# An MoE and attention block on one core: the second tile's upper experts moved from step 11 to step 9, their gating from step 11 to step 10

## The reference

```python
xn = _layernorm(x)
# attention: 16 heads of 8 features, causal
q, k, v = (xn @ W.T + b for each of Wq, Wk, Wv)
scores = einsum('bhqd,bhkd->bhqk', q, k) / sqrt(8)
attn = softmax(where(causal, scores, -inf))
a = einsum('bhqk,bhkd->bhqd', attn, v) @ Wo.T + bo
# experts: the best 2 of 8, weighted by the softmax of their two logits
top_val, top_idx = top_k(einsum('btd,ed->bte', xn, gate_w), 2)
y_all = einsum('btd,edm->btem', xn, We)
e = sum(y_all at top_idx * softmax(top_val))
out = x + a + e
```

## Time and profile before

| what | value |
|---|---|
| median of 3 runs | 516.22 us |
| span of the profiled execution | 510.5 us |
| PE busy | 477.8 us, 94% |
| VectorE busy | 420.7 us, 82% |
| ScalarE busy | 396.9 us, 78% |
| GpSimd busy | 345.9 us, 68% |
| share of PE in the chain that ended last | 89% |

### The profile page before, as it was taken

One profiled execution on the slowest core, in us unless ns is written; L12 is line 12 of the kernel. 1 busy time (PEld: TensorE's weight loads), 2 busy tenths in 40 slices (PEclk: granted clock), 3 DMA queues, 4 the chain that ended last, 5 costly groups with the idle time before them and its releaser, 6 DMA issues.

```text
span 510.5 us, 17312 instructions
## 1 busy us (share of the span) xinstructions
PE 477.8 (94%) x6274; PEld 393.8 (77%) x6274; DVE 420.7 (82%) x1111; ACT 396.9 (78%) x1062; POOL 345.9 (68%) x561
## 2 busy tenths in 40 slices
PE   2548799999999999999999999999999999999995
PEld 1437688888888888888888888888888888888863
DVE  5897698888888898888888898888888898888721
ACT  3644688888888888888888888888888888887773
POOL 7264657777777777778777777777777777755443
PEclk9999999999999999999999999999999999999999
DMA  4664746656547566655465566655556566552000
GB/s 124 195 140 117 188 122 152 161 136 156 134 119 162 130 151 156 160 139 145 105 168 128 148 154 160 156 141 143 139 128 147 138 152 161 133 132 44 15 13 22
DMA packets 64281, 67.79 MB, mean 133 GB/s; under 512 B 6828, under 2 KB 59180, under 8 KB 59484
## 3 DMA queue, kind: packets, MB, share of 16 engines
q1 hardware_dynamic: 64196, 66.68, 53.0%
HBM read 44.90 MB, written 21.23 MB: 130 GB/s over the span
## 4 chain that ended last, share of the span: by engine, by line
PE 89%; DVE 3%; ACT 3%; DMA 2%; issue 2%; SPq 0%; POOL 0%; DVEq 0%; POOLq 0%; ACTq 0%
PE m L841 23%; PE oT_ps L911 17%; PE scoreT_ps L887 13%; PE score_ps L867 12%; PE scoreT_ps L892 5%; PE score_ps L861 5%; PE m L953 3%; PE m L996 3%; PE m L1014 3%; PE m L926 2%; PE m L1021 1%; PE m L962 1%; DMA qstack<-mT 1%; ACT probs L499 1%; DVE negmax L625 1%
## 5 line engine op out<-in xcount | busy, mean ns | idle before, releaser
L625 DVE TENSOR_REDUCE negmax<-score_ps 128x2 f32<-128x512 f32 (+1 forms) x384 | 249.7, 678 | 46.4 <-PE score_ps L867 43.7
L499 ACT ACTIVATE probs<-scoreT_ps 128x512 f32<-128x512 f32 x384 | 216.5, 603 | 74.2 <-PE scoreT_ps L887 48.0
L394 POOL TENSOR_TENSOR fours<-lower,upper 128x512 f32<-128x512 f32 x64 | 81.7, 1276 | 54.1 <-ACT upper L549 54.1
L841 PE MATMUL m<-we_hl,xnT_hl 128*128 128x512 f32 x384 | 114.6, 420 | 0.0
L867 PE MATMUL score_ps<-kstack,qstack 72*128 72x128 bf16 (+1 forms) x1024 | 103.8, 224 | 5.6 <-DVE negmax L625 5.5
L887 PE MATMUL scoreT_ps<-qstack,kstack 123*128 123x128 bf16 (+1 forms) x1024 | 102.0, 221 | 3.3 <-DMA qstack<-mT 2.6
L911 PE MATMUL oT_ps<-probs,vaug 128*32 128x256 f32 (+1 forms) x2048 | 96.7, 329 | 0.2 <-ACT probs L499 0.2
L887 PEld LDWEIGHTS scoreT_ps<-qstack,kstack 123*128 123x128 bf16 (+1 forms) x1024 | 68.1, 98 | 26.5 <-ACT probs L499 15.4
L911 PEld LDWEIGHTS oT_ps<-probs,vaug 128*32 128x32 f32 x2048 | 57.3, 109 | 29.1 <-ACT probs L499 0.4
L549 ACT ACTIVATE upper<-m,weight 128x128 f32<-128x128 f32 x256 | 73.1, 376 | 8.2 <-PE m L841 8.2
L867 PEld LDWEIGHTS score_ps<-kstack,qstack 72*128 72x128 bf16 (+1 forms) x1024 | 72.1, 100 | 8.8 <-DVE negmax L625 7.6
(11 more groups left out here) (81 smaller groups left out, 649.7 us busy)
## 6 DMA issues: line engine op xcount, KB each, us to landing
kstack<-scratch SPq DMA_DIRECT2D x93, 192.0 KB
scratch<-parts SPq DMA_DIRECT2D x64, 192.0 KB, 2.4
qstack<-scratch SPq DMA_DIRECT2D x62, 192.0 KB
qstack<-scratch SPq DMA_DIRECT2D x31, 256.0 KB
x_sb<-in_x SPq DMA_DIRECT2D x32, 128.0 KB, 2.3
scratch<-parts SPq DMA_DIRECT2D x32, 128.0 KB, 1.9
out<-out_sb SPq DMA_DIRECT2D x32, 128.0 KB, 3.7
qstack<-mT SPq DMA_DIRECT2D x64, 8.0 KB, 2.1
```

The lines of the kernel that those rows point to most:

```text
L394: g.tensor_tensor(fours[:, :, q, :], lower[:, :, q, :], upper[:, :, q, :], ALU.add).then_inc(pool_sum, 1)
L499: a.activation(o, i, ACT.Exp, scale=SCALE).then_inc(act_exp, 1)
L625: v.tensor_reduce(o, score_ps[n % 2][:].rearrange("p (h k) -> p h k", h=w), axis=AX.X, op=ALU.max, negate=True).then_inc(dve_max, 1)
L841: ins = tn.matmul(o, l, r, start=first, stop=l is low)
```

## The change

Two places change. On PE the product of the upper experts of the second tile, `experts(mix, 3)`, stood in step 11 behind `turn_input` and ahead of the output projection; now it stands in step 9, directly behind `experts(mix, 2)`. It keeps its wait for the first tile's gating by ACT (`act_upper`), which frees bank `m2`. On ACT the gating of that product, `upper_experts(mix, 1)`, stood in step 11 between `copy_input` and `round_input`; now it stands at the head of step 10.

```diff
@@ ACT, slot(t, s) @@
                     if n == 11 and has(s, NXT):
                         copy_input(t + NXT)
-                    if n == 11 and has(s, -1):
+                    if n == 10 and has(s, -1):
                         upper_experts(mix, 1)
                     if n == 11 and has(s, NXT):
                         round_input(t + NXT)
@@ PE, slot(t, s) @@
                     if n == 9 and has(s, -1):
                         pe.wait_ge(dve_lower, upto(mix, per=2, k=1))
                         experts(mix, 2)
+                        pe.wait_ge(act_upper, upto(mix, per=2, k=1))
+                        experts(mix, 3)
                     if n == 11 and has(s, NXT):
...
                         turn_input(t + NXT)
-                    if n == 11 and has(s, -1):
-                        pe.wait_ge(act_upper, upto(mix, per=2, k=1))
-                        experts(mix, 3)
                     if n == 11 and has(s, -2):
                         pe.wait_ge(act_oTn, upto(fin))
```

## The result

The changed kernel takes 565.33 us (median of 4 runs, 564.19 to 566.87), against 516.92 us for the kernel before, of which there are now four runs: a ratio of 1.0944, 95% interval 1.0912 to 1.0975. The forecast was 565 us.

A forecast was written before the change was run, and what follows sets the result against it. PE was taken as the bound; 41.0 (slots 2 to 28) + 5.4 (29 to 31) + 1.7 (32) + 0.5 (slot 1) = 48.6 us on 516.2 gave 565 us, range 556 to 579, chance 0.80.

The forecast's parts named there:

- PE had no slack: Mid-program slots: PE busy 14.40 of 14.40 us, so any wait of PE costs its whole length.
- The rival by which modelled ends of matmuls hide slack: At the projection: hidden PE slack over 1.5 us a slot absorbs the wait; 514 us, chance 0.04.
- The join is worth nothing: Six expert products together on PE at step 9: -0.01 to +0.01 us a slot, taken as 0.
- the rule for sustained streams: Skill page's 131 ns per 512-column matmul; would save some 21 us over 31 slots, not used in the sum.
- The path over ScalarE: Step 9's transposed scores to projection's end: 3.15 us against 1.63 of PE work, 1.52 us stall a slot.
- One sign: Expected in the profile after: PE's busy time stays near 477.8 us.
- No second stall: Next slot's value product (L953): input halves ready 0.38 us before PE; rival second wait 580 us, chance 0.11.
- Slot 32: Slot without scores, where PE already waits for exponentials: 1.7 us more.
- a rival with 0.02 for a quarter of every slot: TensorE drops to 1.2 GHz for 3.6 us of each slot: 112 us more, 677 us, chance 0.02.
- The start: Slot 1, no projection but a later xnT copy: 0 to 1.0 us, taken as 0.5.
- the 5.7 us "around the span": Median of timed runs 516.22 us less profiled span 510.5 us, taken as time lying around the span.
- the middle: Slots 2 to 28: 27 stalls of 1.52 us, 41.0 us together.

The follow-up runs named there:

- PE's part: Only the upper experts' product moved to step 9 on PE, gating left at step 11, against the kernel before: 531.38 us, ratio 1.0316.
- the gatings behind oTn: Changed kernel with its four gatings still in step 10 but after the oTn copy: 552.20 us, 1.0716 to the kernel before.
- ScalarE's part alone: Only the gating moved to step 10 on ScalarE, product left at step 11 on PE, against the kernel before: 599.04 us, ratio 1.1646.

## Why the prediction was right

**PE had no slack.** True: the slot grew by the wait, 1.54 us, and nothing of it was taken up elsewhere. The rival by which modelled ends of matmuls hide slack is gone with that.

**The join is worth nothing.** True on PE: 1.46 us before and after. By the rule for sustained streams that the forecast weighed (131 ns a matmul, Trainium skill, TensorE: Matmul & The Clock Gate, section "Back-to-back issue gap") the six would take an estimated 0.79 us; the measurement decides, 243 ns each.

**The path over ScalarE.** True in order and size: 3.17 us against 3.15, and four gatings cost twice what two cost. Both edits were needed for the whole: PE's part takes away 0.70 us of cover and costs 0.52 alone, ScalarE's adds 1.02 us to the path. One sign missed: PE's busy time was to stay near 477.8 us and is 486.4. A full slot has 14.63 us of it and not 14.40, as the projection behind the stall takes 0.71 in place of 0.45 us; the path counted that, the sign did not.

**No second stall.** True for the changed kernel: the halves are done at 234.92, and PE, behind 0.92 us of its own pieces, comes to the value product at 235.42.

```profile
234.50 0.42 DVE L678 TENSOR_TENSOR xnT_hl<-m,xnT_high 128x256 fp32r<-128x256 f32 x1
```

The margin is 0.50 us, where 0.38 was worked out; the run with the gatings behind oTn used it up.

**Mis-sized terms.** Slot 32 was worked out at 1.7 us and took 3.9; the granted clock is 0.50 in five of its microseconds, which the forecast had as a rival with 0.02 for a quarter of every slot, and not as a small sum at the ends. The start took 3.4 in place of 0.5: in the chain the DMA that PE waits for there landed 1.7 us later than before, and the other 1.6 us came behind that stop at the lower clock. In the ten other kernels the same point is reached between 64.9 and 68.8 us, in no order that follows what they lose in their slots. And the 5.7 us "around the span" are not that: the profiled execution after has a span of 564.0 and a time of 566.2, 2.2 us apart, so the profiled execution of before was 3.5 us or more below the median of its runs. It had a mean granted clock of 0.998, that of after 0.978. In the 36 runs of the kernel before beside the experiments, those at 0.997 and above took 512.2 to 513.8 us, those at 0.983 and below 514.5 to 517.1. Some of the 5 us by which the span grew more than the medians therefore belongs to the two executions and not to the change; how much, no run shows. So the middle, 41.5 against 41.0 us, bears the forecast out, while it is partly luck that the medians differ by 48.4 us where 48.6 were forecast: two terms at the ends were mis-sized by 5 us in the profile, and a quick profiled execution of before stands against them.

## What to carry to other kernels

Where one engine is full, read which other engine's work stands beside each of its pieces before moving one: the piece that moves may be the cover of a copy that nobody was seen to wait for. For each instruction put ahead of others in an in-order queue, follow what stands behind it there until the full engine needs it, and add that path up from the last event that starts it. In these runs, moving one late result forward moved the wait to the next one. More cover brought 0.2 us a slot back once and nothing the second time; less work for the helper engine was not tried.

## What the runs showed of the hardware

What PE's granted clock did behind stops differs within these runs. At the program's start, before, a stop of 2.6 us, most of which the earlier trace rows show, was followed by 1.00; in the changed kernel a stop of 2.8 us at the same place was followed by 0.52 in the next 2.5 us. With ScalarE's part alone, stops of 2.0 us in every slot were followed by 1.00 in most slots and by 0.55 for 3.8 us in about every fourth. Stops of 1.3 us in every slot, in the changed kernel, left it at 1.00 in all full slots.
